# Block powers and block scores of four groups as row tiles of 32, 8 and 4 rows into four banks of one ring

## The reference

```python
ck = k.reshape(B, nh, nblocks, BLOCK, hd).mean(axis=3)      # BLOCK 32, nblocks 32, nh 16, hd 8
cv = v.reshape(B, nh, nblocks, BLOCK, hd).mean(axis=3)
compressed_out = _attn(q, ck, cv)
imp = jnp.einsum('bhqd,bhkd->bhqk', q, ck) * scale
block_scores = jax.nn.softmax(imp, axis=-1).sum(axis=2)      # sum over the 1024 queries
_, idx = jax.lax.top_k(block_scores, TOPK)                   # TOPK 8 of 32 blocks
```

## Time and profile before

| | us |
|---|---|
| median of 3 runs | 3876.97 |
| their range | 3868.96 to 3891.06 |
| the profiled execution's own time | 3863.82 |
| its span, first to last instruction | 3862.0 |
| TensorE / VectorE / ScalarE busy in the span | 3192.9 / 2807.8 / 2308.1 |
| mean granted TensorE clock (of 2.4 GHz) | 0.866 |

### The profile page before, as it was taken

One profiled execution on the slowest core, in us unless ns is written; L12 is line 12 of the kernel. 1 busy time (PEld: TensorE's weight loads), 2 busy tenths in 40 slices (PEclk: granted clock), 3 DMA queues, 4 the chain that ended last, 5 costly groups with the idle time before them and its releaser, 6 DMA issues. The chain is left out here.

```text
span 3862.0 us, 92355 instructions
## 1 busy us (share of the span) xinstructions
PE 3192.9 (83%) x38480; PEld 1472.6 (38%) x38480; DVE 2807.8 (73%) x4293; ACT 2308.1 (60%) x3868; POOL 1239.8 (32%) x1018
## 2 busy tenths in 40 slices
PE   6999999899867777689979888887995676876799
PEld 2222222256511121156633233333543564654445
DVE  8898899587779999977755677756445667657643
ACT  3888888766554555356643377775645555543565
POOL 1101100045537786735534010001005665552100
PEclk7999999999967788799989899988996666656799
DMA  4101010100010010010036112201000000000000
GB/s 104 29 9 29 14 24 8 33 6 2 11 33 17 17 28 22 17 34 2 2 61 95 18 27 38 39 23 50 1 10 3 4 4 4 4 3 3 31 9 15
DMA packets 136037, 84.90 MB, mean 22 GB/s; under 512 B 92386, under 2 KB 107283, under 8 KB 135491
## 3 DMA queue, kind: packets, MB, share of 16 engines
q1 hardware_dynamic: 132870, 74.71, 9.0%
q0 software_dynamic: 2688, 4.20, 0.7%
q10 hardware_dynamic: 64, 0.07, 0.0%
HBM read 47.23 MB, written 18.33 MB: 17 GB/s over the span
## 5 line engine op out<-in xcount | busy, mean ns | idle before, releaser
L997 DVE TENSOR_REDUCE attn_peak_halves<-attn_ps 128x2 f32<-128x1024 f32 x512 | 601.6, 1219 | 55.2 <-PE attn_ps L828 47.6
L950 ACT ACTIVATE attn_weights<-attn_ps 128x512 f32<-128x512 f32 x1024 | 531.1, 601 | 97.9 <-PE attn_ps L856 97.8
L1258 POOL TENSOR_TENSOR moe_hidden<-moe_exact,moe_hidden 128x512 f16<-128x512 f32 x256 | 297.2, 1165 | 331.7 <-ACT moe_hidden L1242 323.3
L3707 POOL TENSOR_TENSOR delta_q<-delta_q,delta_weighted 128x512 f32<-128x512 f32 x240 | 325.2, 1382 | 236.5 <-ACT delta_weighted L4101 236.2
L254 PE MATMUL moe_ps<-moe_xT_halves,moe_w_halves 128*128 128x512 f16 x1536 | 364.0, 384 | 9.2 <-DVE moe_w_halves L1275 5.9
L3005 DVE TENSOR_REDUCE sparse_peak<-sparse_ps 128x4 f32<-128x1024 f32 x256 | 299.3, 1219 | 93.9 <-PE sparse_ps L2632 93.9
L1793 POOL TENSOR_TENSOR mamba_out_c<-mamba_states,mamba_c_rep 128x1024 f32<-128x1024 f32 x128 | 301.7, 2369 | 169.7 <-DVE mamba_states L1860 132.1
L856 PE MATMUL attn_ps<-attn_q_stack,attn_k_stack 50*128 50x512 f16 x1024 | 321.3, 385 | 27.5 <-ACT attn_weights L950 7.1
L254 PE MATMUL ffn_ps<-ffn_layers,ffn_h_halves 128*128 128x512 f16 x1536 | 334.4, 379 | 3.6 <-ACT ffn_gate L3250 3.6
L1579 PE MATMUL mamba_ps<-mamba_stack,mamba_spread 96*128 96x512 bf16 x512 | 196.7, 489 | 136.5 <-DVE mamba_states L1860 74.2
L1860 DVE TENSOR_TENSOR_SCAN mamba_states<-mamba_decays,mamba_ps 128x1024 f32<-128x1024 f32 x128 | 292.7, 2287 | 16.9
(11 more groups left out here) (454 smaller groups left out, 6328.7 us busy)
## 6 DMA issues: line engine op xcount, KB each, us to landing
mamba_stack<-mamba_parts SPq DMA_DIRECT2D x96, 128.0 KB, 2.4
sparse_factor<-sp_factor SPq DMA_DIRECT2D x24, 256.0 KB
sp_halves<-sparse_parts SPq DMA_DIRECT2D x8, 512.0 KB, 3.0
ffn_h<-in_h SPq DMA_DIRECT2D x4, 1024.0 KB, 8.0
attn_q_stack<-attn_halves SPq DMA_DIRECT2D x96, 32.0 KB
attn_k_stack<-attn_halves SPq DMA_DIRECT2D x96, 32.0 KB
attn_halves<-attn_hp SPq DMA_DIRECT2D x8, 384.0 KB, 3.1
attn_q_stack<-attn_peak_rows SPq DMA_DIRECT2D x128, 2.0 KB
```

The lines of the kernel that those rows point to most:

```text
L950: act.activation(weights[:, at % 2, h, :], use.slot, ACT.Exp).then_inc(*key_act.one())
L997: dve.tensor_reduce(peak_halves[:, turn % PEAKS, keys, at:at + 2], use.slot, AX_X, ALU.max).then_inc(*score_dve.one())
L1258: pool.tensor_tensor(low, exact_sb[:, i % 3, :], hidden[:, i // EB % 3, i % EB, 0, :], ALU.subtract).then_inc(*hidden_low.one())
L3707: pool.tensor_tensor(so_far, so_far, weighted[:, half, :], ALU.add).then_inc(*long_added.one())
```

## The change

The three kinds of small-contraction matmuls are laid out so that each group uses its own 32 rows of the array. A block power now contracts 32 rows (and its peak matmul 8), a block score 4 rows, each starting at row 32g. The four groups of one half are one piece: four float32 matmuls in a row and then four float16 ones for the powers, four float32 ones for the scores, into four different banks. The constants `peak_spread` and `head_spread` shrink accordingly, and `block_turn` writes its 32 rows as four times 8 rows at 32g, with 16 small matmuls in place of 4.

Each of these pieces takes all four slots of `key_ring` and waits for all four to be empty before its first matmul. The ring therefore has banks 4 to 7 from the beginning, and the clock-keeping matmuls ahead of the attention (`heat`) take a slot of the ring like any other piece, in place of the spare bank. In the schedule, the four `qk` and two `lay` of the next batch, which stood between the groups, now follow the four powers.

```diff
     if use.earlier:
         by, count = use.earlier
-        pe.wait_ge(*empty[by].at(count))
+        if by != "pe":
+            pe.wait_ge(*empty[by].at(count))
...
-            for g in range(GROUPS):
-                yield "block_power", b, 0, g
-                if nxt:
-                    yield "qk", b + 1, g
-                if scored:
-                    yield "block_score", b - 1, 0, g
+            yield "block_power", b, 0
+            if nxt:
+                for i in range(4):
+                    yield "qk", b + 1, i
+            if scored:
+                yield "block_score", b - 1, 0
...
-            for g in range(GROUPS):
-                yield "block_power", b, 1, g
-                if nxt and g < 2:
-                    yield "lay", b + 1, g
+            yield "block_power", b, 1
+            if nxt:
+                for c in range(2):
+                    yield "lay", b + 1, c
             if scored:
-                for g in range(GROUPS):
-                    yield "block_score", b - 1, 1, g
+                yield "block_score", b - 1, 1
                 yield "sum_scores", b - 1
...
         def score_last_blocks(b):
             for half in range(HALVES):
-                for g in range(GROUPS):
-                    yield [("block_score", b, half, g)]
+                yield [("block_score", b, half)]
+                yield from [[] for _ in range(GROUPS - 1)]
...
-            first = [piece for _ in range(units + lead) for piece in (*next_score(), ("warm", 2))]
+            first = [piece for n in range(units + lead) for piece in (*next_score(), ("heat", 2, n))]
             yield from among(first, [("block_keep", B - 1)], pick_blocks(B - 2))
-            yield "warm", 10
-            yield ("widen",)
+            yield "heat", 10, units + lead
...
-        key_ring, uses = Ring(banks(ps, 3, 4)), {}
+        key_ring, uses = Ring(banks(ps, 4, 4)), {}
...
-                 "block_power": (key_ring, "act", 1), "block_out": (key_ring, "act", 1), "block_invert": (key_ring, "dve", 1),
-                 "block_score": (key_ring, "dve", 1), "lay_scores": (key_ring, "dve", 1),
-                 "locate": (key_ring, "dve", 1), "split": (key_ring, "act", 1), "score": (score_ring, "dve", 1),
+                 "block_power": (key_ring, "act", GROUPS), "block_out": (key_ring, "act", 1), "block_invert": (key_ring, "dve", 1),
+                 "block_score": (key_ring, "dve", GROUPS), "lay_scores": (key_ring, "dve", 1),
+                 "locate": (key_ring, "dve", 1), "heat": (key_ring, "pe", 1),
+                 "split": (key_ring, "act", 1), "score": (score_ring, "dve", 1),
...
                     for j in range(TPC):
-                        made = pe.matmul(use.slot[0:2 * HEADS, tile(j)], block_peak_parts[:, TPC * half + j].rearrange(
-                            "p h s -> p (h s)"), ident_half[:], start=True, stop=True)
+                        for g in range(GROUPS):
+                            heads = slice(GROUP * g, GROUP * (g + 1))
+                            made = pe.matmul(use.slot[of_head(g, 2 * GROUP), tile(j)],
+                                             block_peak_parts[:, TPC * half + j, heads].rearrange("p h s -> p (h s)"),
+                                             ident_half[:], start=True, stop=True)
...
-                def block_power(b, half, g):
-                    use = one("block_power", b, half, g)
+                def block_power(b, half):
+                    mine = uses["block_power", b, half]
                     pe.wait_ge(*key_act.at(one("block_turn", b, half).over))
-                    wait_empty(pe, use, key_empty)
-                    pe.matmul(use.slot, mean_rows[:, b % 2, tile(g)], q_value[:, b % 2, columns(half)],
-                              start=True, stop=False)
-                    pe.matmul(use.slot, peak_spread[:, g, :], block_peak_rows[:, columns(half)], start=False,
-                              stop=True).then_inc(*key_full.one())
+                    for use in mine:
+                        wait_empty(pe, use, key_empty)
+                    for g, use in enumerate(mine):
+                        rows = of_head(g, 32)
+                        pe.matmul(use.slot, mean_rows[rows, b % 2, tile(g)], q_value[rows, b % 2, columns(half)],
+                                  start=True, stop=False)
+                    for g, use in enumerate(mine):
+                        rows = of_head(g, 2 * GROUP)
+                        pe.matmul(use.slot, peak_spread[rows, :], block_peak_rows[rows, columns(half)], start=False,
+                                  stop=True).then_inc(*key_full.one())
...
-                def score_of_blocks(b, half, g):
-                    use = one("block_score", b, half, g)
+                def score_of_blocks(b, half):
+                    mine = uses["block_score", b, half]
                     pe.wait_ge(*key_dve.at(one("block_invert", b, half).over))
-                    wait_empty(pe, use, key_empty)
-                    pe.matmul(use.slot, head_spread[:, g, :], block_inverse_rows[:, half, :],
-                              start=True, stop=True).then_inc(*key_full.one())
+                    for use in mine:
+                        wait_empty(pe, use, key_empty)
+                    for g, use in enumerate(mine):
+                        rows = of_head(g, GROUP)
+                        pe.matmul(use.slot, head_spread[rows, :], block_inverse_rows[rows, half, :],
+                                  start=True, stop=True).then_inc(*key_full.one())
```

More of the change, by code:

```diff
@@ L113, in __init__ @@
         self.before = [None] * len(slots)
-    def add(self, slot):
-        self.slots.append(slot)
-        self.before.append(None)
     def take(self, by):
@@ L2561, in block_invert @@
                     use = one("block_invert", b, half)
-                    pe.wait_ge(*key_act.at(one("block_power", b, half, GROUPS - 1).over))
+                    pe.wait_ge(*key_act.at(one("block_power", b, half).over))
                     wait_empty(pe, use, key_empty)
@@ L2819, in block_turn, with block_power @@
                     act.wait_ge(*key_full.at(use.n))
[L2820 to L2823 removed]
+                    act.copy(block_peak_rows[:, columns(half)], use.slot).then_inc(*key_act.one())
+                def block_power(b, half):
                     if b >= 2:
[L2825 to L2827 removed]
+                        act.wait_ge(*key_dve.at(one("block_score", b - 2, half).over))
+                    for g, use in enumerate(uses["block_power", b, half]):
+                        act.wait_ge(*key_full.at(use.n))
+                        act.activation(powers[:, b % 2, half, g, :], use.slot, ACT.Exp).then_inc(*key_act.one())
                 def block_output(b, half):
@@ L2864, in keep_sum @@
                     if g == half == 0:
-                        act.wait_ge(*key_dve.at(one("block_score", B - SLOTS + kind, HALVES - 1, GROUPS - 1).over))
+                        act.wait_ge(*key_dve.at(one("block_score", B - SLOTS + kind, HALVES - 1).over))
                     if b and quad == 0:
```

76 lines of the change are left out of this document (36 added, 40 removed).

## The result

| | before | after |
|---|---|---|
| median of 20 runs each, us | 3872.6 | 3883.9 |
| ratio of the runs, 95% interval | | 1.0029 [1.0017, 1.0041] |
| the profiled execution's own time, us | 3863.8 | 3885.5 |
| mean granted clock over the span | 0.866 | 0.859 |

The account below looks back on a forecast made before the run. Preparation bound by TensorE in its first two thirds, VectorE in the last. Walk -10.7, attention +2, clock +12 give +3 us: 3867 against the profiled execution's 3863.8, 3880 against the median; range 3852 to 3901.

Parts of the forecast that it names:

- Forecast A: Whole kernel: no measurable change, between -9 (no clock cost) and +9 us, 3868 to 3886, likeliest 3880; chance 0.63.
- The tiles: Powers and scores: row tiles overlap fully, four powers with peaks take 1.3 us; TensorE's total relief about 50 us.
- Rival D: Powers and scores: the tiles do not overlap and all waits come on top, +41 us, 3918; chance 0.06.
- The waits for four banks: Preparation: pieces wait for the whole ring, TensorE idles nearly 4 us behind the reciprocal in batches 1, 2 and 3.
- the walk: Hand timing of the preparation's batches at full clock: batch 2 ends 1.9 us earlier, all batches 10.7 us earlier.
- Rival C: Whole kernel: TensorE sets it all and its share counts fully, -50 + 2 + 8, 3837 us; chance 0.06.
- The clock: Preparation: falls to 1.2 GHz after the new waits cost 12 us, bounds 0 and 25.
- Rival E: Preparation stays at 1.2 GHz, clock 0.5 for more than half of the batch: +21 us, 3898; chance 0.11.
- The attention's first steps: Batch 3's scores at the attention's start: waiting for four exponentials loses 1 us on each half, 2 us in all.
- The units: Score units made in advance after the preparation: the wait ahead of them, ring and order there stay as before.
- rival B: Units made in advance: new timing spares the clock's fall, 9 to 10 us more gain; with A's good end -19, 3858; chance 0.14.
- The fourth bank: Batch 0 of the preparation: 0.4 us more gain for the gates, which now have four banks.

Follow-up runs that it names:

- e1: The kernel after, with all float32 powers and scores contracting 128 rows again instead of row tiles; 1.0068 of before.
- e3: The kernel after, plus 12 dense matmuls under VectorE's reciprocal ahead of the first powers of batches 1 to 3; 0.9988 of before.
- e7: e6 without the two dense clock-keeping matmuls beside each score unit made in advance; 0.9929 of before in six runs.
- e6: The kernel after, with each matmul of a set waiting for its own bank only, plus e3's dense matmuls under the reciprocal; 0.9962 of before.
- e10: e5 without the two dense matmuls beside each unit made in advance, no row tiles; 0.9981 of before.
- e5: The kernel before, with the ring of four banks from the beginning and `heat` in place of `warm`, no tiles or new order; 0.9971 of before.
- e11: e7 unchanged, run again on another chip; 0.9943 of before in twelve runs.

## Why the prediction was right, point by point

Forecast A named 3880 us, no measurable change, and 3883.9 was measured. Against the runs of before the sum said +3 us and +11 was measured, so the forecast has the sign, and two sizes were off. As a difference, +11 lies just outside A's own -9 to +9. The time fell inside 3868 to 3886, and within 4 us of 3880, because the median of before, 3877.0 in three runs, came down to 3872.6 in twenty: that part is luck.

**The tiles (right).** Four float32 matmuls start within 0.02 us and hold TensorE for 0.93 us against 3.61 for e1's; powers with peaks 1.35 us, forecast 1.3. The figure of the Trainium skill, TensorE: Matmul & The Clock Gate, section Measured speedup vs the span model, gave an estimated 1.12 us where the prediction took 0.86 plus a change of shape; the trace has 0.93, a factor of 3.9, and the row is what decides. Rival D (no overlap) is out. Its price, +41 us, was too high as well: e1 is that rival built, but for the peak matmuls, and lies 26 us above before. Its low-clock time is 23.9 us and not 71.7, and part of its longer matmuls is hidden behind the other engines; the two were not separated.

**The waits for four banks (right, in place and in size).** The wait behind the reciprocal came three times, 3.58, 3.67 and 3.42 us (forecast nearly 4). The table under e3 shows the walk step by step: what was forecast as 1.9 us earlier is 2.5 in e3's batch 2. In all, most of the 50 us of TensorE time bring nothing at full clock, as said, because VectorE and ScalarE between TensorE's pieces set the rest. Rival C (all 50 us count) is out for that reason.

**The clock (the step whose size was wrong).** The prediction put 12 us, with bounds 0 and 25. By stretches that end at the second reciprocal of each batch:

| | batch 0 | batch 1 | batch 2 | batch 3 | sum |
|---|---|---|---|---|---|
| forecast, walk and clock | -3.7 | +1.6 | +1.9 | +1.5 | +1.3 |
| after minus before | -2.2 | +2.6 | +5.3 | -0.8 | +4.9 |

In batch 2, 3.8 us of clock were forecast, and 8.0 were measured between e3 and after. The reason is in the clock, which the forecast let recover behind each wait: it took "one to two `qk`" as slow. In the trace the low stretch that begins at 2069.0, already ahead of the long wait and behind one of 1.53 us, lasts 13.7 us, and the next from 2086.1 lasts 17.0, through `v`, powers, `lay`, scores and peaks, the first four of them with waits of 0.8 to 1 us ahead. The small waits do not do it alone: in e3 nearly the same ones stand in batch 2 (0.79, 0.95, 0.84, 0.95 us), with the long one filled, and only 3.4 us of the batch are low. So what the forecast missed is a low stretch that lasts over the long wait and on, and a second one behind it; why the second comes is open.

At 0.35 us for each microsecond at the low clock, an estimate from e3 and after, the 65 us more than before cost 23, near the upper bound of the forecast, 25; the walk at full clock would then be worth -18, not -10.7. By the same estimate the walk is -3.4, -3.5, -4.1 and -6.8 us for the four batches, against -4.2, -2.2, -1.9 and -2.4: most of the difference stands in batch 3, which has 20.5 of its 29.1 us at the low clock and is still 0.8 us shorter than before. Whether its walk was so much better or the low clock is cheaper there is open. Measured is the sum, which was off by 3.6 us.

Rival E, with a clock of 0.5 for more than half of a batch, comes out in batch 2 (28.9 of 44.9 us between the reciprocals) and in batch 3 (20.5 of 29.1), not in batch 1 (18.9 of 42.5). So its sign was there in two batches of three, and its +21 was 10 too high for the whole all the same: batch 3, where it had put +6, came out shorter than before.

**The attention's first steps (right in sign, low in size).** The first 32 exponentials took 34.3 us on average in the five traces with single scores for the last batch, and 36.9 in the nine with sets of four: 2.6 us, forecast 2. The two groups overlap (33.3 to 35.7 and 34.4 to 38.2). TensorE waits 1.75 us and 1.25 us ahead of the two sets, and the sets run at the low clock. The whole attention is 4.5 us longer on average (460.9 to 465.5) in those traces; what the 1.9 us beyond the first steps are was not tried, and one program's attention varies by more.

**The units (forecast: no change; right).** 34.3 and 34.7 us. The wait that rival B hoped to lose is there as before, 2.20 us (was 2.21). Of B's 9 to 10 us some 4 to 6 can be had in the units, but by leaving out the dense matmuls beside them (e7 against e6, e10 against e5). Against B's way by the clock speaks e5: TensorE waits 0.55 us there and not 2.2, and the units run at 0.50 all the same.

**The fourth bank (0.4 us in the prediction).** For the kernel after nothing speaks against it. What the prediction missed is that the change carried in it an edit which alone gives 11 us, 0.9971 of before, so the rest of the change costs some 22 us and not 11. The earlier trace rows had the sign of it. The prediction took the wait of 2.32 us in front of a score only as one that was there before. That score reads the first reciprocal, which had ended near 2105; what it waited for was the bank that the second one still read, and with a fourth bank the score runs under the second, and the power behind it waits 1.09.

**What would show it.** TensorE's busy share between 2034 and 2110 fell from 96% to 80%, not 65%: the rest of the fall is hidden in matmuls that take about twice as long at the low clock (sets of 2.09 us, not 1.14). The stretch from reciprocal to reciprocal in batch 2 did not "hardly shrink", it grew by 5.3 us.

**What lies outside the stage.** The delta-rule layer, with the same instructions in all kernels, took 727 to 748 us in fourteen traces, with 468 to 521 us of it at the low clock; after's had 737.7, before's 729.3. No cause in the change was found, and no order by kernel. This range of 21 us is as large as the effects under study, and the reason why the verdicts above rest on medians and the mechanism on the stage alone.

## To carry over

- When several pieces become one that takes every slot of a ring, count which pieces ran in the shadow of the slowest reader of a slot. Here a wait in front of each instruction, in place of one in front of all four, gave back 13 us (13.7 in the preparation) without anything else.
- Price a new gap on TensorE by the whole stretch at the lower clock that may follow it, not by the next one or two pieces: with one wait of 3.67 us in it and small ones behind, 28.9 of a batch's 44.9 us were low. Filling the gaps of about 3.5 us with dense matmuls was worth 4 us each; two such matmuls per unit, where TensorE itself sets the pace, cost 0.7 us per unit.
- Take an edit apart and time each half: the best version (0.993 to 0.994 of before) keeps the tiles and the fourth bank, waits bank by bank, covers the reciprocals and drops the idle matmuls beside the units.

## Not expected of the hardware

- The clock stayed at 0.50 for 17.0 us (2086.1 to 2103.1 of after) while TensorE was busy 13.88 of them, with gaps of 0.8 to 1 us between the pieces. Nearly the same gaps in e3 stood at the full clock. In e5 single powers and scores without such gaps held 1.00 for nearly the whole preparation (0.2 us low).
- In the units, two dense matmuls in each 1.85 us did not lift the clock from 0.50; it was 0.50 without them too.
- Between equal traces of one kernel (e7, e11) the stretches at the low clock lie elsewhere, and the preparation differs by 4.4 us for it.
